# A graph network's last three aggregations: which chunks are fetched row by row, and by whom

## The chip, the cores and the metric

The program runs on one core of a Trainium2 chip. Its time is device microseconds; the number used is the median of three runs. An engine is named as the profile names it: PE (TensorE), PEld (its weight loads), DVE (VectorE), ACT (ScalarE), POOL (GpSimd), SP (SyncE); a q behind the name (ACTq, SPq) is that engine's queue of register, semaphore and DMA-issuing instructions.

## The reference, cut to what matters

3125 nodes with 256 features, 50000 edges sorted by destination. Two attention layers, an edge-attribute layer, then a relational layer and two hypergraph convolutions. The last three end in the same form: rows of a table, one for each edge, are fetched by the edge's source, weighted, and added up by destination.

```python
# relational layer: table rows are (source node, relation)
msg = h[edge_src] * edge_norm[:, None]
agg = jax.ops.segment_sum(msg, seg, num_segments=R * N)
# each of the two convolutions
h = jax.nn.relu(x @ w1 + b1)
msg = ew[:, None] * h[src]
agg = jax.ops.segment_sum(msg, dst, num_segments=x.shape[0])
h = agg @ w2 + b2
```

Both layers become: fetch 50000 rows of 256 floats from HBM (`rel_d` once, `feat_d` twice), and add them up per destination node.

## The kernel before, in words

**Tiling.** Edges are cut into chunks of 128; two chunks are a pair, and there are 196 pairs (`PAIRS`). A pair's rows land in one of 28 ring slots (`ring`, `RING`), edge p of a chunk in partition p. TensorE multiplies a pair by a 0/weight matrix that DVE makes, once for every destination tile that the pair touches: 220 steps (`T`) for 196 pairs. DVE adds each step's result to the tile's sum. In the last 21 or so steps PE also does the work of the layer that follows, for tiles that are finished (`pe_rows_late`, `pe_convolve_late`).

**Who fetches.** POOL walks the pairs (`gather_pairs`, L181) and issues one indirect DMA for each chunk (L186). For every pair from 28 on it waits until `slot_free` says that the slot is free; the wait for pair u is passed when ACT has begun its note of pair u - 25. In 12 of the pairs, 14, 28, ... 168 (`BY_ROW`), POOL fetches the first chunk alone; the second chunk's 128 rows are fetched one by one with plain DMAs of 1 KB (`fetch_row`, L203 to 207), rows 0 to 63 by SP (`sp_gather_rows`, L209) and rows 64 to 127 by ACT (`act_gather_rows`, L223). Each such engine first loads up to 32 row addresses (`ROW_REGS`) from SBUF into registers with one load (L219 on SP, L246 on ACT), and then issues one DMA for each.

**Notes.** For pairs 0 to 171 (`NOTES` = 172) ACT tells PE that a pair is there: it waits until the steps of an old pair are done (that number comes from `lastT`, of which L229 loads 14 entries, `LASTS`, every 14 pairs), frees the slot (L232), waits for the pair's landing and in a by-row pair for its 128 rows, and counts `pair_ready` up (L237). Behind each note it issues a share of the rows for the next by-row pair: 64 rows over 14 notes, the last of them right before that pair's own note. From pair 172 on POOL gives the notes itself (`pool_note`, L196), that of pair u - 2 behind the fetches of pair u; before the first of these, at pair 174, it waits until all of ACT's 172 notes are given (L199).

**SP.** For by-row pair number n it waits for the slot (as POOL does), and from n = 2 on for all rows of number n - 2 (L215), then loads and issues 64 rows. It has nothing else to do meanwhile.

The addresses of the rows lie in `row_rel` and `row_src`, one partition for each by-row pair, 128 four-byte entries in it; `lastT` is one row of four-byte entries. Row 64 of a chunk thus stands 256 bytes behind the start of its partition's addresses, and entry 14 of `lastT` 56 bytes behind its start.

Of the kernel before, what the change touches and what calls it, by code (L numbers as in the profile page):

```python
# [14 lines left out]
P = 128  # L15
# [22 lines left out]
BIG = 1.0e30  # L38
LN_EPS = 1e-5
BN_EPS = 1e-5  # L40
ROW_STEP = 14
NOTES = 172
PEEL = 2
SAFE = PAIRS
ACT_TILES = 10
BY_ROW = tuple(range(ROW_STEP, NOTES, ROW_STEP))
SP_ROWS = 64
ROW_REGS = 32
ROW = 4 * D
LASTS = 14  # L50
W_GAT = D + HEADS + 1
DX = D + 2 * HEADS
AW = 130
# [20 lines left out]
def pool_chunks(u, gat, by_row):  # L74

    return 1 if u in by_row or (u == PAIRS - 1 and not gat) else 2


class Signal:
# [7 lines left out]
def gnn_program(nc, t, out):  # L87
    life = ExitStack()

    def sb(name, shape, dt=F32, scope=None):  # L90
        return (scope or life).enter_context(nc.sbuf_tensor(name, shape, dt))
# [64 lines left out]
    class Steps:  # L156


        def __init__(self, tag, scope, gat, attr=None, signals=sem, by_row=()):
            self.gat, self.attr, self.width = gat, attr, W_GAT if gat else D  # L160
            self.by_row = by_row
            if by_row:
                self.rows_landed = [signals(f"{tag}_rows_landed{k}") for k in range(2)]
            self.hot_made = signals(tag + "_hot_made")
            self.pair_ready = signals(tag + "_pair_ready")
            self.step_done = signals(tag + "_step_done")
            self.slot_free = signals(tag + "_slot_free")
            self.added = signals(tag + "_added")
            if attr is not None:
                self.attr_hot_made = signals(tag + "_attr_hot_made")  # L170
                self.attr_ready = signals(tag + "_attr_ready")
                self.attr_done = signals(tag + "_attr_done")
                self.attr_added = signals(tag + "_attr_added")
                self.attr_landed = [signals(f"{tag}_attr_landed{k}") for k in range(4)]
            self.landed = []
            for u in range(PAIRS):
                at = pair_landed[u % RING]
                at.at += 16 * pool_chunks(u, gat, by_row)
                self.landed.append(at.at)

    def gather_pairs(pool, g, table, index, ring, pairs=range(PAIRS)):  # L181
        for u in pairs:
            if u >= RING:
                pool.wait_ge(g.slot_free, u - RING + 1 + RELEASE)
            for j in range(pool_chunks(u, g.gat, g.by_row)):
                pool.indirect_dma_start(  # L186
                    out=ring[:, u % RING, j, 0:D], out_offset=None, in_=table,
                    in_offset=bass.IndirectOffsetOnAxis(ap=index[:, u, j:j + 1], axis=0),
                ).then_inc(pair_landed[u % RING].sem, 16)
            if not g.gat and u - 2 >= NOTES:  # L190
                pool_note(pool, g, u - 2)
        if not g.gat:
            for u in range(PAIRS - 2, PAIRS):
                pool_note(pool, g, u)
# [8 lines left out]
    def fetch_row(eng, g, n, p, at, table, ring):  # L203

        row = bass.RuntimeValue.of_register_unchecked(at, min_val=0, max_val=(table.shape[0] - 1) * ROW)
        eng.dma_start(ring[p:p + 1, g.by_row[n] % RING, 1, 0:D].bitcast(U8),
                      table.rearrange("n f -> (n f)").bitcast(U8)[bass.ds(row, ROW)].unsqueeze(0))           .then_inc(g.rows_landed[n % 2], 16)

    def sp_gather_rows(sp, tag, g, table, index, ring):  # L209

        for n, u in enumerate(g.by_row):
            if u >= RING:
                sp.wait_ge(g.slot_free, u - RING + 1 + RELEASE)
            if n >= 2:
                sp.wait_ge(g.rows_landed[n % 2], 16 * P * (n // 2))  # L215
            for q in range(0, SP_ROWS, ROW_REGS):
                w = min(ROW_REGS, SP_ROWS - q)
                at = [sp.alloc_register(f"{tag}_at{n}_{q + k}") for k in range(w)]
# [4 lines left out]
    def act_gather_rows(act, tag, g, table, index, ring):  # L223

        lasts = [act.alloc_register(f"{tag}_last{k}") for k in range(LASTS)]
        done = act.alloc_register(f"{tag}_done")
        for u in range(NOTES):
            if u % LASTS == 0:
                act.reg_load(lasts, lastT[0:1, u:u + LASTS])  # L229
            act.reg_alu(done, lasts[u % LASTS], 1, ALU.max)  # L230
            act.wait_ge(g.step_done, done)
            act.sem_inc(g.slot_free, 1)  # L232
            act.wait_ge(pair_landed[u % RING].sem, g.landed[u])
            if u in g.by_row:
                n = g.by_row.index(u)
                act.wait_ge(g.rows_landed[n % 2], 16 * P * (n // 2 + 1))
            act.sem_inc(g.pair_ready, 1)  # L237
            n, share = u // ROW_STEP, u % ROW_STEP
            if n < len(g.by_row):
                rest = P - SP_ROWS  # L240
                for k in range(rest * share // ROW_STEP, rest * (share + 1) // ROW_STEP):
                    p = SP_ROWS + k
                    if k % ROW_REGS == 0:
                        w = min(ROW_REGS, P - p)
                        at = [act.alloc_register(f"{tag}_at{n}_{p + x}") for x in range(w)]
                        act.reg_load(at, index[n:n + 1, p:p + w])  # L246
                    fetch_row(act, g, n, p, at[k % ROW_REGS], table, ring)

    def ready_pairs(act, tag, g, ring):
        lasts = [act.alloc_register(f"{tag}_last{k}") for k in range(RING)]  # L250
# [162 lines left out]
    ring = sb("ring", [P, RING, 2, W_GAT], scope=gat)  # L413
# [25 lines left out]
    def carve(area, at, shape, dt=F32):  # L439

        size = 1
        for n in shape:
            size *= n
        size //= {BF16: 2, U8: 4}.get(dt, 1)
        flat = area[:, at:at + size]
        flat = flat if dt == F32 else flat.bitcast(dt)
        names = " ".join("abcd"[:len(shape)])
        return flat.rearrange(f"p ({names}) -> p {names}", **dict(zip("abcd", shape))) if len(shape) > 1 else flat
# [54 lines left out]
    rest = carve(arena_flat, 5490, (2 * HEADS * NT,))  # L503
# [1126 lines left out]
    def tail():  # L1630
# [272 lines left out]
        with nc.Block() as block:  # L1903
            @block.sync
            def _(sp):
                chunk = ROW_STEP * 2 * P
                for goal, ids in ((row_src, t["src"]), (row_type, t["type"])):
# [44 lines left out]
            @block.scalar  # L1952
            def _(act):
                act.wait_ge(s_row_at, 1)
                act_gather_rows(act, "agr", g_rel, rel_d, row_rel, ring)
                act.wait_ge(s_eps, 1)
                act_rows(act)
                for z, tag in enumerate(convs):
                    for k in range(5):
                        act.wait_ge(stored[k], 16 * 5 * (z + 1))  # L1960
                    act_gather_rows(act, f"ag{tag}", g_conv[z], feat_d, row_src, ring)
                    act_convolve(act, z)
                    act_sqrt(act, z, 0)
                    for r in range(NR):
                        act_norm(act, z, 0, r, s_n1[z], ACT.Relu)
                    act_sqrt(act, z, 1)
                    for r in range(NR):
                        act_norm(act, z, 1, r, s_n2[z], ACT.Identity if z else ACT.Relu)
                        if z == 1 and r >= 2:
                            for n in range(CH[r - 2][0] + 1, CH[r - 2][1], 2):  # L1970
                                act_odd(act, n)
                        if z == 0 and r >= 2:
                            for n in range(*CH[r - 2]):
                                act_rectify(act, 1, n)
                    if z == 0:
                        for n in range(CH[NR - 2][0], NT):
                            act_rectify(act, 1, n)
                for n in range(CH[NR - 2][0] + 1, NT, 2):
                    act_odd(act, n)
# [100 lines left out]
```

## Time and profile before

| what | value |
|---|---|
| three runs | 3306.64, 3307.64, 3316.96 us; median 3307.64 us |
| span of the profiled execution | 3318.0 us |
| busiest | POOL 2386.1 us (72%), PE 2189.3 us (66%), DVE 2090.3 us (63%), ACT 1413.4 us (43%) |
| mean granted TensorE clock | 0.844 |
| DMA | 466.05 MB, mean 140 GB/s |

The profile is one execution. The span is from its first to its last instruction; of the three runs the slowest lies nearest to it. The three aggregations that the change touches are three stretches of some 475 us each: 1765.8 to 2241 us, 2259.2 to 2734.5 us and 2789.8 to 3265 us. A row of the page's groups names line, engine, operation, what is written and read, the count, then busy time, mean ns of one, and the idle time before them with what ended it. Waiting, loading of registers and issuing of plain DMAs are not counted as busy, so ACT and SP look idle in these stretches; what their queues do is seen in the views of single lines and in the timeline.

### The profile page before, as it was taken

What the parts mean: (1) busy time and instruction counts of PE and PEld (TensorE: products, weight loads), DVE (VectorE), ACT (ScalarE), POOL (GpSimd) and SP (SyncE); (2) the same over time, 40 slices, a digit from 0 to 9 for tenths busy, and PEclk for the clock granted to TensorE, in tenths of its full rate; (3) what the DMA queues carried; (4) which work ended last, traced back from release to release, by engine and by line L of the source; (5) the groups of instructions that cost most, each with busy time, mean ns of one, the idle gap of its engine ahead of it and who ended that gap; (6) DMA issues with size and microseconds to landing.
All of it is one profiled execution on the core that took longest, in us unless ns stands there. A gap on an engine that the chain in (4) does not pass through costs nothing. (4 is left out here: it accounts for less than half of the span.)

```text
span 3318.0 us, 73877 instructions
## 1 busy us (share of the span) xinstructions
PE 2189.3 (66%) x11487; PEld 1592.8 (48%) x11488; DVE 2090.3 (63%) x5467; ACT 1413.4 (43%) x4736; POOL 2386.1 (72%) x2419
## 2 busy tenths in 40 slices
PE   6566377776656367766696666676666677666667
PEld 2455255555455355555443444454444456444446
DVE  8899867766489967776694444464444454444446
ACT  2666399998566479988581000031000014000004
POOL 7877777777777767777655777775777773777773
PEclk9799699998889789999797778687777798777788
DMA  5488734443688745443694333443333332333332
GB/s 165 132 228 226 215 111 141 140 127 105 174 227 227 214 118 163 142 130 104 161 283 159 109 109 109 125 125 108 109 109 109 108 104 78 110 109 110 109 107 79
DMA packets 346744, 466.05 MB, mean 140 GB/s; under 512 B 111879, under 2 KB 262248, under 8 KB 343184
## 3 DMA queue, kind: packets, MB, share of 16 engines
q0 software_dynamic: 111952, 284.59, 29.8%
q1 hardware_dynamic: 161584, 111.23, 11.5%
q10 hardware_dynamic: 72852, 67.08, 7.5%
q14 instruction: 328, 2.69, 0.3%
q8 instruction: 28, 0.46, 0.1%
HBM read 385.50 MB, written 76.97 MB: 139 GB/s over the span
## 5 line engine op out<-in xcount | busy, mean ns | idle before, releaser
L400 PE MATMUL t_ps<-t_ring,shared 128*128 x2640 | 900.5, 494 | 499.2 <-ACTq L237 418.3
L400 PEld LDWEIGHTS t_ps<-t_ring,shared 128*128 128x128 f32 x2640 | 601.8, 244 | 787.5 <-issue 697.4
L186 POOL DMA_INDIRECT ring<-feat_d,srcC x784 | 772.3, 985 | 264.8 <-issue 215.2
L186 POOL DMA_INDIRECT t_ring<-feat_d,srcC x758 | 719.7, 950 | 289.3 <-issue 215.5
L265 ACT ACTIVATE ring<-ring,exC 128x64 f32<-128x64 f32 x3136 | 788.0, 335 | 0.2
L400 PE MATMUL bank<-ring,arena 128*128 x1408 | 426.9, 428 | 166.7 <-ACT ring L265 117.8
L318 DVE TENSOR_TENSOR acc<-acc,t_ps 128x256 f32 x440 | 185.3, 421 | 504.3 <-PE t_ps L400 502.9
L608 POOL DMA_INDIRECT attr_d<-abuf,attr_pos x392 | 401.9, 1025 | 117.7 <-issue 117.7
L186 POOL DMA_INDIRECT t_ring<-rel_d,relC x379 | 360.0, 950 | 160.6 <-issue 107.4
L302 DVE TENSOR_SCALAR shared<-lane,dlocT,weightT 128x128 f32<-128x128 f32 x1320 | 406.4, 360 | 50.9 <-issue 31.9
L1828 ACT COPY t_ring<-t_pt 128x512 f32<-128x512 f32 (+1 forms) x14 | 7.8, 554 | 883.3 <-PE t_pt L1795 883.3
L400 PEld LDWEIGHTS bank<-ring,arena 128*128 128x128 f32 x1408 | 258.5, 204 | 240.0 <-issue 213.3
L1036 PE MATMUL wide<-arena 128*128 128x100 bf16 x4704 | 258.0, 215 | 173.5 <-ACT arena L952 157.9
L1036 PEld LDWEIGHTS wide<-arena 128*128 128x128 bf16 x4704 | 232.6, 102 | 199.5 <-DVE arena L997 118.3
L296 DVE TENSOR_TENSOR arena<-lane,dlocT 128x256 f32<-128x256 f32 x440 | 185.0, 420 | 91.1 <-issue 53.4
L318 DVE TENSOR_TENSOR X<-X,t_ps 128x256 f32 x220 | 92.5, 420 | 234.0 <-PE t_ps L400 232.7
L318 DVE TENSOR_TENSOR acc<-acc,bank 128x261 f32 x352 | 150.2, 427 | 117.0 <-PE bank L400 108.4
L948 ACT ACTIVATE arena<-arena,minus_part 128x512 bf16<-128x512 bf16 x196 | 141.4, 721 | 146.9 <-issue 116.2
L1003 DVE TENSOR_TENSOR arena<-wide,shared 128x800 f32<-128x800 f32 x196 | 191.2, 976 | 8.9 <-PE wide L1036 8.2
L1768 ACT ACTIVATE rstd<-mv,t_eps 128x1 f32<-128x1 f32 x25 | 7.1, 284 | 439.1 <-DVE mv L1737 439.1
L1012 DVE TENSOR_REDUCE shared<-arena 128x800 f32 (+1 forms) x196 | 190.4, 971 | 0.1
L390 PEld LDWEIGHTS bank<-arena 128*128 128x128 f32 x704 | 139.8, 202 | 70.1 <-issue 45.3
(297 smaller groups left out, 2715.3 us busy)
## 6 DMA issues: line engine op xcount, KB each, us to landing
arena<-lo_d ACTq DMA_DIRECT2D x392, 128.0 KB
rel_d<-mid_stage SPq DMA_DIRECT2D x25, 1024.0 KB, 4.7
arena<-attr_d SPq DMA_DIRECT2D x98, 260.0 KB, 2.9
abuf<-in_attr SPq DMA_DIRECT2D x56, 448.0 KB
t_ring<-feat_d SPq DMA_DIRECT2D x1536, 1.0 KB
t_ring<-feat_d ACTq DMA_DIRECT2D x1536, 1.0 KB
ring<-feat_d,srcC POOLq DMA_INDIRECT x784
t_ring<-rel_d SPq DMA_DIRECT2D x768, 1.0 KB
```

Of the source, the lines that this page charges most:

```text
L186: pool.indirect_dma_start(out=ring[:, u % RING, j, 0:D], out_offset=None, in_=table, in_offset=bass.IndirectOffsetOnAxis(ap=index[:, u, j: ...
L265: last = act.activation(part_of_row, part_of_row, ACT.Copy, scale=exC[:, bass.ds(u, 1), j, h])
L296: last = dve.tensor_tensor(hot[:, k % NHOT, :, :], lane[:, :].unsqueeze(1).to_broadcast([P, 2, P]), dlocT[:, bass.ds(s, 1), :].rearrange(" ...
L302: last = dve.tensor_scalar(hot[:, k % NHOT, j, :], lane[:, :], dlocT[:, bass.ds(s, 1), j], weightT[:, bass.ds(s, 1), j], ALU.is_equal, ALU ...
L318: dve.tensor_tensor(acc[:, tile, 0:g.width], acc[:, tile, 0:g.width], ps[k % len(ps)][:, 0:g.width], ALU.add).then_inc(g.added, 1)
L390: pe.matmul(ps_a[k % NHOT][:, 0:AW - 1], hot_a[:, k % NHOT, :], aring[:, slot, 0:AW - 1], start=True, stop=True).then_inc(g.attr_done, 1)
L400: last = pe.matmul(ps[k % len(ps)][:, 0:g.width], hot[:, k % NHOT, j, :], ring[:, slot, j, 0:g.width], start=(j == 0), stop=(j == 1))
L608: pool.indirect_dma_start(out=attr_d, in_=abuf[:, g % BUFS, k, :], in_offset=None, out_offset=bass.IndirectOffsetOnAxis(ap=attr_pos[:, c:c ...
L948: act.activation(apart[:, k % 2, :], lo[:, k, 1, :], ACT.Abs, bias=minus_part[:, 0:1])\
L1003: dve.tensor_tensor(cand[:, k % 2, :, :, :], pk[k % 2][:, :, :].rearrange("p b (s x) -> p (b s) x", x=P)[:, :, 0:HEADS * NT] .rearrange("p ...
L1012: dve.tensor_reduce(e[:, bass.ds(4 * c, 4), :], cand[:, k % 2, :, :, :].rearrange("p (j q) h n -> p j h q n", q=2), AX.XY, ALU.add).then_i ...
L1036: last = pe.matmul(pk[k % 2][:, j // 2, at:at + HEADS * NT], looked[:, k % 2, q, j * P:(j + 1) * P], tab[:, piece, q * HEADS * NT:(q + 1) ...
```

## The change

By-row pairs are every 12th: 12, 24, ... 168, 14 of them where there were 12, so POOL issues 377 fetches in an aggregation where it issued 379. Of a chunk's 128 rows SP fetches rows 0 to 69 and ACT rows 70 to 127. ACT spreads its 58 rows over the 12 notes that end four notes ahead of the by-row pair's own note (`ROW_LEAD`), and those of the first by-row pair over notes 0 to 7. `lastT` is loaded 16 entries at a time. Addresses are still loaded up to 32 at a time, from the first row that the engine fetches: on SP three loads a chunk (32, 32 and 6, from rows 0, 32 and 64), on ACT two (32 and 26, from rows 70 and 102).

```diff
--- before.py
+++ after.py
@@ -38,16 +38,17 @@
 BIG = 1.0e30
 LN_EPS = 1e-5
 BN_EPS = 1e-5
-ROW_STEP = 14
+ROW_STEP = 12
 NOTES = 172
 PEEL = 2
 SAFE = PAIRS
 ACT_TILES = 10
 BY_ROW = tuple(range(ROW_STEP, NOTES, ROW_STEP))
-SP_ROWS = 64
+SP_ROWS = 70
+ROW_LEAD = 4
 ROW_REGS = 32
 ROW = 4 * D
-LASTS = 14
+LASTS = 16
 W_GAT = D + HEADS + 1
 DX = D + 2 * HEADS
 AW = 130
@@ -74,6 +75,17 @@
 def pool_chunks(u, gat, by_row):
 
     return 1 if u in by_row or (u == PAIRS - 1 and not gat) else 2
+
+
+def act_rows(by_row, u):
+
+    rest = P - SP_ROWS
+    for n in range(len(by_row)):
+        first = max(0, ROW_STEP * n - ROW_LEAD)
+        pairs = ROW_STEP * (n + 1) - ROW_LEAD - first
+        for k in range(rest):
+            if first + k * pairs // rest == u:
+                yield n, k
 
 
 class Signal:
@@ -235,16 +247,13 @@
                 n = g.by_row.index(u)
                 act.wait_ge(g.rows_landed[n % 2], 16 * P * (n // 2 + 1))
             act.sem_inc(g.pair_ready, 1)
-            n, share = u // ROW_STEP, u % ROW_STEP
-            if n < len(g.by_row):
-                rest = P - SP_ROWS
-                for k in range(rest * share // ROW_STEP, rest * (share + 1) // ROW_STEP):
-                    p = SP_ROWS + k
-                    if k % ROW_REGS == 0:
-                        w = min(ROW_REGS, P - p)
-                        at = [act.alloc_register(f"{tag}_at{n}_{p + x}") for x in range(w)]
-                        act.reg_load(at, index[n:n + 1, p:p + w])
-                    fetch_row(act, g, n, p, at[k % ROW_REGS], table, ring)
+            for n, k in act_rows(g.by_row, u):
+                p = SP_ROWS + k
+                if k % ROW_REGS == 0:
+                    w = min(ROW_REGS, P - p)
+                    at = [act.alloc_register(f"{tag}_at{n}_{p + x}") for x in range(w)]
+                    act.reg_load(at, index[n:n + 1, p:p + w])
+                fetch_row(act, g, n, p, at[k % ROW_REGS], table, ring)
 
     def ready_pairs(act, tag, g, ring):
         lasts = [act.alloc_register(f"{tag}_last{k}") for k in range(RING)]
```

## Rows read from the trace of the kernel before

**Rows 1.** Busy time by stretch: the three aggregations (the first and the third; columns as in the first row).
```profile
core 0: us, PE busy (x) PEld busy (x) DVE busy (x) ACT busy (x) POOL busy (x), PEclk, DMA share, GB/s
1765.70:2241.10 475.40, 315.48 (x969) 216.59 (x970) 223.34 (x738) 26.25 (x91) 359.97 (x379) 0.77 0.40 115
2789.70:3265.00 475.30, 315.19 (x969) 216.99 (x970) 210.51 (x670) 10.04 (x20) 359.82 (x379) 0.77 0.38 108
```

**Rows 2.** Line 186 (POOL) in the third aggregation: one line's view, durations in ns.
```profile
L186 POOL DMA_INDIRECT t_ring<-feat_d,srcC x379: 942/947/1031, 2789.8 to 3264.0; - x190
  issue: 107.7, 353
```

**Rows 3.** The same view, only as far as pair 174.
```profile
L186 POOL DMA_INDIRECT t_ring<-feat_d,srcC x338: 942/947/1031, 2789.8 to 3212.5; - x169
```

**Rows 4.** Who waited for whom: total us, times, longest us.
```profile
PE t_ps L400 <- ACTq L237: 418.3, 236, 10.7
POOL t_ring L186 <- ACTq L232: 22.0, 72, 0.3
...
SPq L219 <- ACTq L232: 250.6, 33, 10.4
```

**Rows 5.** Chain that ended last, around the end of the third aggregation: start, us, what.
```profile
3246.50 0.95 POOL t_ring L186
...
3249.31 1.12 PE t_ps L400 x4
...
3276.16 0.48 ACT t_ring L1837
```

**Rows 6.** Line 237 (ACT notes) at both ends of the third aggregation.
```profile
L237 ACTq EVENT_SEMAPHORE  x1: 17/17/17, 2793.8 to 2793.8; - x1
...
L237 ACTq EVENT_SEMAPHORE  x2: 17/17/17, 3205.2 to 3207.8; - x2
```

**Rows 7.** Line 206 (row fetches) in the third aggregation.
```profile
L206 ACTq DMA_DIRECT2D t_ring<-feat_d x768: 227/228/544, 2796.2 to 3200.3; - x192
```

**Rows 8.** Timeline of ACT's queue, three short stretches: start us, us, what, count.
```profile
2338.26 1.50 ACTq L206 DMA_DIRECT2D t_ring<-feat_d  x5
...
2353.24 3.01 ACTq L206 DMA_DIRECT2D t_ring<-feat_d  x9
...
2336.53 1.10 ACTq L206 DMA_DIRECT2D t_ring<-feat_d  x3
```

**Rows 9.** Timeline of SP's queue, one chunk, then its second half.
```profile
2343.51 23.27 SPq L206 DMA_DIRECT2D t_ring<-feat_d  x64
...
2356.52 10.26 SPq L206 DMA_DIRECT2D t_ring<-feat_d  x32
```

**Rows 10.** Line 229 (14 registers each): all, then four single loads.
```profile
L229 ACTq TENSOR_LOAD <-lastT x39: 1228/1577/3477, 1767.7 to 3200.6; - x39
...
L229 ACTq TENSOR_LOAD <-lastT x1: 3317/3317/3317, 1804.6 to 1804.6; - x1
...
L229 ACTq TENSOR_LOAD <-lastT x1: 1507/1507/1507, 1839.8 to 1839.8; - x1
...
L229 ACTq TENSOR_LOAD <-lastT x1: 3312/3312/3312, 3167.0 to 3167.0; - x1
...
L229 ACTq TENSOR_LOAD <-lastT x1: 1515/1515/1515, 3200.6 to 3200.6; - x1
```

**Rows 11.** Other register loads: 4, 20, 28, 32 and 32 registers each.
```profile
L362 DVEq TENSOR_LOAD <-tiles x5: 345/347/355, 842.9 to 3262.2; - x5
...
L381 PEldq TENSOR_LOAD <-slots x55: 1357/1362/1582, 409.4 to 3223.2; - x55
...
L253 ACTq TENSOR_LOAD <-lastT x14: 1717/1738/1931, 412.2 to 1543.7; - x14
...
L219 SPq TENSOR_LOAD <-t_row_src x48: 2024/2119/2281, 2258.5 to 3155.7; - x48
...
L246 ACTq TENSOR_LOAD <-t_row_src x48: 1968/2066/2162, 2263.3 to 3184.9; - x48
```

## The prediction

> **What bounds the kernel now.** I read the busy time by stretch first. In each of the three aggregations POOL is the busiest engine at 360 of 475 us, PE follows at 309 to 315, and ACT looks idle [rows 1]. Then the view of POOL's own line. Its 379 fetches start between 2789.8 and 3264.0 us, one every 474.2 / 378 = 1.2545 us. A fetch takes 0.947 us, and the 353 gaps behind "issue" are 107.7 / 353 = 0.305 us each, which adds up to the same 1.252 us [rows 2]. So POOL never stops, and an aggregation lasts 379 x 1.2545 = 475.4 us plus a tail. The waits agree. POOL's 22.0 us behind ACT's slot count are 72 times 0.3 us, the ordinary gap under another name; SP by contrast waits 250.6 us for slots, and PE waits 418.3 us for ACT's notes, since it is fed at POOL's pace [rows 4]. The chain shows POOL up to some 3249 us, then PE until ACT takes over at 3276.2 [rows 5]. That last stretch of PE work (late steps and the next layer's products) hangs on POOL's last pairs and is not touched, so the tail stays as it is.
>
> The views of single lines show the second thing to be read: how near ACT's queue is to POOL's pace. It counts as idle and is not. In the third aggregation its first note ends at 2793.8 and its last at 3207.8 [rows 6], that is 4.0 and 418.0 us after POOL's start. POOL's own first note comes behind pair 174, at 338 x 1.2545 = 424 us [rows 3]; there it waits until ACT is through. ACT now arrives 6 us before that. This is the point where a late ACT turns into a late POOL.
>
> **What the queue steps cost.**
> Row fetch on ACT: five DMAs span 1.50 us, and the last is 0.23 long, so the pitch is (1.50 - 0.23) / 4 = 0.318 us [rows 7, 8]. Nine with a note between them span 3.01 us, so a note that has nothing to wait for costs 3.01 - 0.23 - 8 x 0.318 = 0.24 us; other such stretches give 0.22, and I take 0.225 [rows 8]. The first fetch behind a load takes longer: three span 1.10 us in place of 0.87, 0.23 us more [rows 8].
> Row fetch on SP: (10.26 - 0.23) / 31 = 0.324 us; with its load in the middle a chunk of 64 takes 23.27 us [rows 9].
> Register loads: 4 registers take 0.35 us, 20 take 1.36, 28 take 1.74, 32 take 2.0 to 2.15 [rows 11]. That is about 0.25 us for every four.
> The 14-register load of line 229 does not fit. Of its 39 executions 21 take 1.23 to 1.60 us and 18 take 3.29 to 3.48, and they alternate: 3317, 1507 ... 3312, 1515 ns [rows 10]. They differ in nothing but the address. The quick ones begin 0, 112, 224 ... bytes into the row, the slow ones 56, 168 ... bytes, and these are 8 more than a multiple of 16. My reading: from an address that is a multiple of 16 four registers are read at a time (14 are then three fours and two single ones, five reads, as 20 registers are five fours). From any other address each register is read alone, at 3.315 / 14 = 0.237 us. All loads of rows 11 begin at multiples of 16 (20 registers are 80 bytes, 28 are 112, rows 32, 64 and 96 stand at 128, 256 and 384 bytes).
> The Trainium skill, page "Runtime: NRT & Kernel Launch", section "Instruction fetch mechanics", says that a load into sequencer registers costs about 200 ns a register even in bulk. The slow loads agree (0.237 us), the aligned ones do not (0.065 us). With 0.20 for 0.237 the sum below would be 14 x 58 x 0.037 = 30 us smaller an aggregation, some 3481 us in all.
>
> **The change part by part.**
> POOL: two fetches fewer an aggregation, 2 x 1.2545 = 2.5 us, three times 7.5 us. This is all that can be gained while POOL is the bound.
> lastT 16 at a time: entries 0, 16, 32 ... stand at multiples of 64 bytes, so 11 loads of four fours, between 1.0 and 1.5 us, taken as 1.1 (between the rows of 4 and of 20 registers, nearest to the latter). Before, 13 loads averaged some 2.4 us. It saves about 19 us of ACT's queue.
> SP: 70 x 0.325 + 2.05 + 2.14 for two loads, about 0.8 for the one of 6 registers at row 64 (256 bytes, three reads), 0.2 for the rest: 28 us a chunk. By-row pairs come every 23 fetches x 1.2545 = 28.9 us. SP keeps up just so. It starts up to 25 pairs early, and even 2.1 us for the short load (29.3 us, 0.4 us lost a chunk) stays inside that lead. Cost: nothing; that lead hides it.
> ROW_LEAD: the last row comes four notes before its pair's note, so the note no longer waits for it. That moves waiting off ACT only.
> ACT's address loads: this is what decides. Its rows now begin at 70, 280 bytes in, and at 102, 408 bytes in. Both are 8 more than a multiple of 16. No row of the trace shows 32 registers from such an address. From below the price is that of an aligned load, 2.06 us [rows 11]; next comes that price plus the whole difference of line 229 as a fixed toll, 2.06 + 1.8 [rows 10]; from above it is each register alone at 0.245. I take each alone at 0.237, because that one rule gives all five sizes of rows 10 and 11: 32 x 0.237 = 7.6 and 26 x 0.237 = 6.2 us, 13.7 us a chunk where 4.1 were.
>
> **The sum.** ACT from POOL's first fetch to its last note, when it never waits: 4.0 to the first note; 14 x 58 = 812 rows x 0.318 = 258.2; 28 first fetches x 0.23 = 6.4; 14 x 13.74 = 192.4; 10 further lastT loads x 1.1 = 11.0; 171 notes x 0.225 = 38.5. Together 510.5 us. The same sum for the kernel before (768 rows, 24 loads of 2.06, six lastT loads of 3.3 and six of 1.5) gives 371, and its last note is at 418.0, so 47 us of waiting for landings are in there. They are slack, and a late ACT doesn't have them.
> POOL comes to its own first note behind 336 fetches, at 421.5 us, and stands until 510.5. (From about pair 90 on it will also be held by the ring, when ACT is some 24 pairs late; that time is inside the same 89 us.) Then 41 fetches x 1.2545 = 51.4 us follow: 561.9 against 475.4, 86.5 us more an aggregation, 259.5 us for three. By pairs: ACT needs 18.4 + 0.5 + 13.7 + 0.8 + 2.7 = 36.2 us for 12 pairs, POOL 28.9. The stretch behind pair 175 runs at POOL's pace as before, so PE's tail is the same.
> The differences go onto the median: 3307.6 + 259.5 = 3567 us. Against the span of the profiled execution, which is 10.4 us above the median, it would be 3577.5.
>
> **The rivals.**
> 1. Each register alone (the forecast). Single reads of 0.225 to 0.245 us and a pitch of 0.318 to 0.33 give 225 to 300 us more: 3533 to 3608. Chance 0.82.
> 2. The bad address costs a toll on each load and not a toll on each register. ACT's sum with aligned prices is 510.5 - 192.4 + 14 x 4.0 = 374; each us of toll adds 28. POOL is held only beyond 421.5, so from a toll of 1.7 us on. At 1.8 it is 424.6: POOL loses 3.1 and gains 2.5, some 3310 us. At 4 it is 486, 3494 us. For it speaks that only one size was seen at such an address; against it that 3.3 / 14 meets the price that two leftover registers need in rows 10. Chance 0.07.
> 3. Not slower: the address of rows 70 and 102 costs nothing. ACT then needs 26.5 us for 12 pairs against POOL's 28.9, its last note is at some 415 us, before POOL's 421.5, and POOL stays the bound. The time is 3307.6 - 7.5 = 3300.1 us, 0.23% faster. It decides at a load price below 3.7 us in the mean. Against it stand 18 loads of 18. Chance 0.09.
> 4. SP falls behind and holds ACT's notes, because row fetches from both queues at once slow down. At 0.36 us a row SP would need 30.5 us a chunk, 1.6 too much, and ACT's notes would end 20 us late: 3340 us if alone. SP's pitch beside ACT's is 0.324 and steady. Chance 0.02.
>
> **How the numbers follow.** The forecast is case 1, 3567 us. Its bounds and the skill's price for a register give 3481 to 3608; with half of case 2 above the lower end, and room for instruction fetches on a queue that now never rests, the range is 3480 to 3620 and leaves out case 3, most of case 2 and case 4. About 0.3% (10 us) is what a measurement here can tell from no change. Faster by more needs case 3 with something on top: 0.02. Within it: the rest of case 3 and the lowest part of case 2, 0.09. Slower: 0.89.
>
> **What would show it.** L246 at 7.6 and 6.2 us, and L229 near 1.1, all alike. L206 on ACT at an unchanged pitch. ACT's last note 510 us behind POOL's first fetch. POOL's line with waits for L232 of tens of us and one long wait for the notes, at pair 175, and otherwise the same 1.2545 us. SP waiting for slots more than now. PE waiting for L237 some 200 us more. The prediction is wrong if L246 stays near 2 us (then case 3), or takes 4 (case 2), or if POOL waits nowhere.

## The result, and the profile after

The changed kernel takes 3586.7 us (3583.87 to 3588.71 in four runs), the kernel before 3307.1 us (3306.03 to 3316.96 in four). The ratio is 1.0835, with a 95% interval of 1.0814 to 1.0855: 279.6 us slower. The forecast was 3567 us, in a range of 3480 to 3620.

The page of the changed kernel: its span, the busy time of the engines, and the costliest group with the idle time ahead of it.

```profile
span 3583.0 us, 75473 instructions
PE 2173.2 (61%) x11487; PEld 1579.8 (44%) x11488; DVE 2090.6 (58%) x5467; ACT 1413.3 (39%) x4736; POOL 2377.8 (66%) x2413
L409 PE MATMUL t_ps<-t_ring,shared 128*128 x2640 | 885.2, 488 | 791.7 <-ACTq L249 711.2
```

No engine is busy for longer than before by more than 0.3 us. PE's matmuls in the aggregations wait 711.2 us for ACT's notes where they waited 418.3 [rows 4]. The busy time by stretch says how long the first and the third aggregation last from POOL's first fetch to its last:

```profile
core 0: us, PE busy (x) PEld busy (x) DVE busy (x) ACT busy (x) POOL busy (x), PEclk, DMA share, GB/s
1753.90:2322.00 568.10, 309.51 (x971) 211.91 (x972) 223.93 (x738) 26.63 (x91) 357.71 (x377) 0.75 0.34 96
2962.70:3530.80 568.10, 309.86 (x969) 212.51 (x970) 211.01 (x669) 10.04 (x20) 357.40 (x377) 0.75 0.31 91
```

568.1 us where it was 475.4 [rows 1], with the same work in it: POOL busy 357.4 us in place of 359.8. The three stretches add 3 x 92.6 = 278 us, which is the whole of the loss. The stretch before the first aggregation is outside the change, and the two profiled executions differ there by some 12 us the other way, so their spans are only 265 us apart.

The view of POOL's line, now 198, in the third aggregation (durations in ns; below it what ended the engine's idle time, us and times), then the same up to pair 174 and from pair 175 on:

```profile
L198 POOL DMA_INDIRECT t_ring<-feat_d,srcC x377: 940/946/1033, 2962.8 to 3529.8; - x189
  issue: 103.4, 339
  ACTq L244: 61.8, 35
  POOLq L213: 45.0, 1
...
L198 POOL DMA_INDIRECT t_ring<-feat_d,srcC x336: 940/946/1033, 2962.8 to 3433.8; - x168
...
L198 POOL DMA_INDIRECT t_ring<-feat_d,srcC x41: 940/946/972, 3479.7 to 3529.8; - x41
```

A fetch still takes 0.946 us and the ordinary gap is still 0.305 us. Two waits are new. The 35 waits for line 244, the slot count that ACT gives, take 61.8 us where 0.3 us each would be 10.7, 51 us more. And one wait of 45 us stands between the 336th fetch and the 337th. Less the two fetches saved this is 51 + 45 - 2.5, some 93 us, the growth of the stretch. The timeline of POOL shows it (start, length, what, and in brackets the idle time ahead and its releaser):

```profile
3432.51 0.94 POOL L198 DMA_INDIRECT t_ring<-feat_d,srcC  x1 [0.30 <-issue]
3433.76 0.95 POOL L198 DMA_INDIRECT t_ring<-feat_d,srcC  x1 [0.30 <-issue]
3479.70 0.94 POOL L198 DMA_INDIRECT t_ring<-feat_d,srcC  x1 [44.99 <-POOLq L213]
3480.94 0.95 POOL L198 DMA_INDIRECT t_ring<-feat_d,srcC  x1 [0.30 <-issue]
```

Line 213 is POOL's own first note, at pair 174; in front of it POOL waits until all 172 of ACT's notes are given (line 211). The first of ACT's notes and the last three, in the view of line 249, and under them ACT's row fetches:

```profile
L249 ACTq EVENT_SEMAPHORE  x1: 17/17/17, 2966.9 to 2966.9; - x1
...
L249 ACTq EVENT_SEMAPHORE  x3: 17/17/17, 3476.3 to 3478.9; - x3
...
L218 ACTq DMA_DIRECT2D t_ring<-feat_d x812: 227/228/534, 2974.0 to 3472.6; - x163
```

The first note ends 4.1 us behind POOL's first fetch at 2962.8, the last 516.1 us behind it. Before, it was 418.0 [rows 6]. POOL goes on 0.8 us later and needs its 41 fetches as ever. What keeps ACT is in its register loads. These are one load of 32 row addresses and one of 26, then all 28 of the third aggregation, then the 33 lastT loads of all three:

```profile
L255 ACTq TENSOR_LOAD <-t_row_src x1: 6899/6899/6899, 2967.0 to 2967.0; - x1
...
L255 ACTq TENSOR_LOAD <-t_row_src x1: 5864/5864/5864, 2985.3 to 2985.3; - x1
...
L255 ACTq TENSOR_LOAD <-t_row_src x28: 5837/6390/7099, 2967.0 to 3455.5; - x28
...
L241 ACTq TENSOR_LOAD <-lastT x33: 1035/1307/1342, 1755.9 to 3464.1; - x33
```

Where a load of 32 took 2.07 us [rows 11] this one takes 6.9; the median of all 42 of its size is 7.07, that of the 42 of 26 registers 5.90. The lastT load, whose 14-register form went up to 3.48 us every second time [rows 10], is never above 1.35.

The waits, longest in total, of POOL, PE and SP (us in total, times, longest):

```profile
POOL t_ring L198 <- ACTq L244: 179.0, 99, 4.6
POOL t_ring L198 <- POOLq L213: 134.7, 3, 45.0
...
PE t_ps L409 <- ACTq L249: 711.2, 213, 10.7
...
SPq L231 <- ACTq L244: 274.6, 33, 10.4
```

### The profile page after: what moved, and what is told of

Its sections match the earlier page's. It is cut to its first block and busy times, and to the rows that moved or that the text cites. A ratio compares the mean times of both kernels' runs of the same rounds, so it can differ in the third digit from the quotient of the medians.

```text
span 3583.0 us, 75473 instructions
## 1 busy us (share of the span) xinstructions
PE 2173.2 (61%) x11487; PEld 1579.8 (44%) x11488; DVE 2090.6 (58%) x5467; ACT 1413.3 (39%) x4736; POOL 2377.8 (66%) x2413
## 5 line engine op out<-in xcount | busy, mean ns | idle before, releaser
L409 PE MATMUL t_ps<-t_ring,shared 128*128 x2640 | 885.2, 488 | 791.7 <-ACTq L249 711.2
L409 PEld LDWEIGHTS t_ps<-t_ring,shared 128*128 128x128 f32 x2640 | 588.6, 241 | 1078.5 <-issue 996.3
L327 DVE TENSOR_TENSOR X<-X,t_ps 128x256 f32 x220 | 92.6, 421 | 326.7 <-PE t_ps L409 325.2
```

Source lines behind the costliest of these rows:

```text
L327: dve.tensor_tensor(acc[:, tile, 0:g.width], acc[:, tile, 0:g.width], ps[k % len(ps)][:, 0:g.width], ALU.add).then_inc(g.added, 1)
L409: last = pe.matmul(ps[k % len(ps)][:, 0:g.width], hot[:, k % NHOT, j, :], ring[:, slot, j, 0:g.width], start=(j == 0), stop=(j == 1))
```

## The experiments

Names: `a_` starts from the changed kernel, `b_` from the kernel before, `c_` is a further version. Each ratio is against the kernel before on the same chip. Its median there was 3311.4 us for `a_aligned`, `a_half`, `b_act8` and `b_sp8`, 3310.5 for `probe`, `b_lasts16`, `a_lead0` and `c_11`, and 3309.2 for `probe2`, `b_step12` and `c_68`.

### Is it the address of ACT's loads, and nothing else?

`a_aligned`: the same rows on the same engines behind the same notes, but the loads begin at entries 68 and 100.

```diff
-                if k % ROW_REGS == 0:
-                    w = min(ROW_REGS, P - p)
-                    at = [act.alloc_register(f"{tag}_at{n}_{p + x}") for x in range(w)]
-                    act.reg_load(at, index[n:n + 1, p:p + w])
-                fetch_row(act, g, n, p, at[k % ROW_REGS], table, ring)
+                if p == SP_ROWS or p in (68, 100):
+                    lo = max(x for x in (68, 100) if x <= p)
+                    w = min([x for x in (68, 100) if x > p] + [P]) - lo
+                    at = [act.alloc_register(f"{tag}_at{n}_{lo + x}") for x in range(w)]
+                    act.reg_load(at, index[n:n + 1, lo:lo + w])
+                fetch_row(act, g, n, p, at[p - lo], table, ring)
```

> The changed kernel with one thing different: ACT loads the addresses of its rows from entries 68 and 100 (272 and 400 bytes in, multiples of 16; 32 and 28 registers) and leaves the two it doesn't need unused. Same rows, same engines, same notes. Theory (each register is read alone from an address that is no multiple of 16, and ACT's queue thereby holds POOL): loads near 2 us in place of 7.0 and 5.9, ACT's sum 4 + 273 for rows + 56 for loads + 13 + 45 = 391 us, below POOL's 421.5, so POOL is the bound with two fetches fewer: 3307.1 - 7.5 = 3299.6 us. Rival (the 14th by-row chunk, 58 rows over 8 notes at the start, or SP at 28 of 28.9 us hold POOL by themselves): the time stays well above before, 3330 us or more, though the loads are short.

Measured: 3302.7 us, ratio 0.9974 (0.9964 to 0.9983). Its loads of two convolutions, and POOL's line in the third aggregation:

```profile
L256 ACTq TENSOR_LOAD <-t_row_src x56: 1909/2026/2196, 2255.1 to 3165.5; - x56
...
L198 POOL DMA_INDIRECT t_ring<-feat_d,srcC x377: 942/946/1032, 2780.1 to 3251.5; - x189
  issue: 106.2, 348
  ACTq L244: 8.2, 27
```

The loads take 2.0 us, and POOL waits for nothing again: 27 gaps of 0.3 us behind the slot count are the ordinary gap. The other parts of the change together with good addresses make the kernel 0.26% faster, 8.8 us against the kernel before on the same chip, where 7.5 were reckoned for six fetches of POOL. So the whole loss of 280 us, and the gain of 9 us besides, hangs on two addresses. Entries 68 and 100 stand at odd multiples of 16 bytes (272 and 400), so 16 is enough; 32 isn't needed. SP now has as little room as ACT: it works without a pause, one chunk every 28.7 us, where POOL reaches the next by-row pair every 28.9.

`a_half`: as `a_aligned`, with loads at entries 70 (30 registers) and 100 (28): `(68, 100)` becomes `(70, 100)`.

> The changed kernel with one of ACT's two loads put right: 30 registers from entry 70 (280 bytes, not a multiple of 16), 28 from entry 100 (400 bytes, a multiple). Theory: 6.6 + 1.9 = 8.5 us a chunk in place of 12.98, so ACT's last note comes 14 x 4.5 = 63 us earlier, at 453 us, still behind POOL's 421.5; each us of it is a us of POOL: 3586.7 - 3 x 63 = 3398 us. Rival (a load from such an address costs a toll beyond a threshold, or POOL's loss isn't proportional to ACT's lateness): not half of the loss goes, or nearly all.

Measured: 3414.2 us, ratio 1.0317 (1.0301 to 1.0332). POOL's wait for the notes:

```profile
POOL t_ring L198 <- POOLq L213: 110.4, 3, 37.6
...
POOL t_ring L198 <- ACTq L244: 21.4, 70, 0.3
```

This is 16 us above the 3398 us expected. ACT's last note comes at 457 us, not 453, which is 12 of the 16 over three aggregations. POOL's idle time at pair 175 is 37 us; less the two fetches, three times 34.5 us is 103 us, the loss against the kernel before on the same chip (102.8). So the loss is proportional to ACT's lateness. Beyond that single wait POOL isn't held: the 70 gaps behind the slot count are the ordinary 0.3 us.

### Does it need the rest of the change?

`b_act8`: the kernel before, with only ACT's loads cut otherwise, by the same code as above with `(64, 66, 98)`.

> The kernel before, 12 by-row chunks of 64 rows on ACT, with ACT's loads cut otherwise: 2 registers from entry 64, 32 from entry 66 (264 bytes), 30 from entry 98 (392 bytes). Nothing else of the change is in it. Theory: 0.6 + 7.0 + 6.6 = 14.2 us a chunk where 4.2 were, 12 x 10 = 120 us onto the 371 to 385 us that ACT needs without waiting: last note near 505 us, 81 us behind POOL's 424: 3307.1 + 3 x 82 = 3553 us, 3530 to 3570. Rival (the loss belongs to every 12th pair or to the 58 rows ahead of time, and addresses only add to it): 3307 to 3400 us.

Measured: 3586.9 us, ratio 1.0841 (1.0825 to 1.0858). ACT's loads in the convolutions, POOL's waits, and the notes' line:

```profile
L247 ACTq TENSOR_LOAD <-t_row_src x72: 494/6749/7214, 2347.1 to 3457.6; - x72
...
POOL t_ring L186 <- POOLq L201: 156.3, 3, 52.2
POOL t_ring L186 <- ACTq L232: 146.0, 81, 6.5
...
L237 ACTq EVENT_SEMAPHORE  x516: 17/17/1992, 1760.9 to 3479.0; - x172
```

So the loss is there without any other part of the change. It is 34 us above the 3553 us expected and outside the 3530 to 3570, 11 us an aggregation. The notes' line says where most of that is: the wait of a note for something that has not landed goes up to 1992 ns. The kernel before fetches its last rows right before their own note, and the landing of those rows is waited for even when ACT is late; I had reckoned ACT as never waiting. Of the 36 by-row notes 15 waited 1.1 to 2.0 us, and all notes of an aggregation took some 8 us more than where nothing of ACT's own is awaited. The remainder is in terms that the sum had a little too small, as told below for the sum of the prediction.

### Does it matter which engine loads slowly?

`b_sp8`: the same cuts for SP.

```diff
-            for q in range(0, SP_ROWS, ROW_REGS):
-                w = min(ROW_REGS, SP_ROWS - q)
+            for q, w in ((0, 2), (2, 32), (34, 30)):
```

> The kernel before, with the same 10 us a chunk put on SP and not on ACT: 2 registers from entry 0, 32 from entry 2 (8 bytes), 30 from entry 34 (136 bytes). Theory: SP then needs 35.5 us a chunk where by-row pairs come every 33.9, so it is late by 1.6 us a chunk from the third chunk on, 14 us at the last; ACT waits for those rows at pair 168 and its last note comes near 430 us, 6 us behind POOL's 424: 3307.1 + 3 x 6 = 3325 us, against some 3553 for the same load cost on ACT. Rival (load time costs the same wherever it stands, for instance because it takes SBUF's port from POOL): 3500 us or more.

Measured: 3320.4 us, ratio 1.0027 (1.0015 to 1.0039). SP's loads in the convolutions:

```profile
L218 SPq TENSOR_LOAD <-t_row_src x72: 635/6359/6834, 2254.1 to 3193.2; - x72
```

Some 10 us a chunk more cost 2 to 3 us an aggregation on SP (477.4 us from first fetch to last in the mean, before 475.3) and 92 on ACT. That is 9 us in all where 18 were expected: ACT did wait for SP's last rows, but its last note came at 424.5 to 426 us and not at 430. A slow load costs what its queue has no room for. SP had some 8 us a chunk to spare and may start up to 25 pairs ahead of a by-row pair, and behind ACT's loads stand the notes that everybody waits for.

### What does a load cost?

A first try added 48 loads with unused results to SP's queue. They are not in its trace, so it measured nothing but the kernel before over again (3307.4 us).

> The kernel before with 48 register loads more on SP, behind its last row fetch, where it only waits for the output: 1, 2, 4, 8, 16 and 32 registers from entries 0, 1, 2, 3, 4, 8, 12 and 16 of an address row. Theory: from entries 0, 4, 8, 12 and 16 (multiples of 16 bytes) a load reads four registers at a time, 0.25 us a read, so 32 registers take 2.0 us; from entries 1, 2 and 3 each register takes 0.21 to 0.24 us, so 32 take 7 us and 4 take 0.9. Rival a: only the address modulo 8 or 4 matters (entry 2 differs from 1 and 3). Rival b: leading registers are read alone until a multiple of 16 is reached, so that entries 1 to 3 cost under 1 us more at any size. The time of the kernel should not move, since SP has some 130 us to wait there.

`probe2` puts the addresses to use: SP's rows are loaded in another cut for each by-row pair (the eight cuts come around again with the ninth).

```diff
-            for q in range(0, SP_ROWS, ROW_REGS):
-                w = min(ROW_REGS, SP_ROWS - q)
+            cuts = [(0, 1, 33), (0, 3, 35), (0, 2, 6, 14, 30, 62), (0, 1, 5, 13, 29, 61), (0, 3, 7, 15, 31, 63),
+                    (0, 4, 12, 28, 60), (0, 32), (0, 2, 34)][n % 8] + (SP_ROWS,)
+            for q, w in [(a, b - a) for a, b in zip(cuts, cuts[1:])]:
```

> The kernel before with SP's rows loaded in other cuts, another for each by-row pair, so that loads of 1 to 34 registers begin at entries of all four remainders: for number 0 at entries 0, 1, 33; 1 at 0, 3, 35; 2 at 0, 2, 6, 14, 30, 62; 3 at 0, 1, 5, 13, 29, 61; 4 at 0, 3, 7, 15, 31, 63; 5 at 0, 4, 12, 28, 60; 6 at 0, 32; 7 at 0, 2, 34. The addresses are in use, which those of the first such try were not (its 48 loads had no user and are not in its trace). Theory: at a multiple of 16 bytes 4, 8, 16, 32 registers take 0.35, 0.6, 1.1 to 1.3, 2.0 us; at remainders of 4, 8 and 12 bytes alike some 0.21 us a register: 0.9, 1.8, 3.5, 6.9 us. Rival a: the remainder of 8 differs from 4 and 12. Rival b: the registers up to the next multiple of 16 are read alone and the others by four, under 1 us more at any size. The time of the kernel is secondary: SP has 8 us to spare a chunk and spends up to 11 more in seven of twelve, so 3307 to 3330 us.

Measured: 3306.7 us in a single run, as much as before within the spread. The view of the loads' line, seven loads of the second aggregation: 4, 8, 16 and 32 registers from entries 2, 6, 14 and 30, then 8, 16 and 32 from entries 4, 12 and 28.

```profile
L220 SPq TENSOR_LOAD <-t_row_src x1: 1152/1152/1152, 2318.0 to 2318.0; - x1
...
L220 SPq TENSOR_LOAD <-t_row_src x1: 1927/1927/1927, 2320.5 to 2320.5; - x1
...
L220 SPq TENSOR_LOAD <-t_row_src x1: 3531/3531/3531, 2325.5 to 2325.5; - x1
...
L220 SPq TENSOR_LOAD <-t_row_src x1: 6747/6747/6747, 2334.3 to 2334.3; - x1
...
L220 SPq TENSOR_LOAD <-t_row_src x1: 795/795/795, 2428.0 to 2428.0; - x1
...
L220 SPq TENSOR_LOAD <-t_row_src x1: 1312/1312/1312, 2431.5 to 2431.5; - x1
...
L220 SPq TENSOR_LOAD <-t_row_src x1: 2216/2216/2216, 2438.1 to 2438.1; - x1
```

All 156 loads together, medians by the remainder of the address (entry modulo 4) and the number of registers, in ns:

| registers | entry mod 4 = 0 | 1 | 2 | 3 |
|---|---|---|---|---|
| 4 | 520 | 1092 | 1149 | 1123 |
| 8 | 795 | 1948 | 1932 | 1928 |
| 16 | 1237 | 3580 | 3539 | 3535 |
| 32 | 2129 | 6763 | 6745 | 6753 |

From 8 to 32 registers an aligned load grows by 1334 ns, 0.22 us for every four registers; the others grow by 4813 to 4825 ns, 0.20 us for each. Both rivals fall: the remainders of 4, 8 and 12 bytes cost alike, and the load doesn't read its way to the next multiple of 16 first. The Trainium skill's page "Runtime: NRT & Kernel Launch", section "Instruction fetch mechanics", gives some 200 ns a register; this is the slope of the loads that start anywhere else, and four registers for that price is what an aligned start gives here. The Trainium skill's page "SBUF — State Buffer", section "Specifications (TRN2)", tells of lines of 16 bytes, the same unit; that the loader reads in such lines is my reading and is shown by no run.

### What are the other parts worth?

`b_lasts16`: the kernel before with `LASTS = 16`.

> The kernel before with the lastT loads of the change alone: 16 entries every 16 notes. Theory: 11 loads of 1.33 us where 13 averaged 2.45 take 17 us off ACT's queue, which then waits those 17 us longer for landings; POOL is the bound, so the time stays at 3311 within 3 us. Rival (ACT's queue holds something up in the kernel before as well): up to 3 x 17 us faster, 3260.

Measured: 3309.9 us, ratio 0.9999 (0.9989 to 1.0008): no difference that can be told, as expected, on a queue that has time to spare.

`b_step12`: the kernel before with `ROW_STEP = 12`.

> The kernel before with the chunk count of the change alone: every 12th pair, rows split 64 and 64 (so ACT's loads stay on multiples of 16 bytes), the last rows right before the note, lastT 14 at a time. Theory: ACT needs 4 + 896 rows x 0.336 + 28 x 2.1 + 29 + 45 = 437 us, and some 1.5 us of landing at each of 14 by-row notes: 458 us, 37 behind POOL's 421; 3310.5 + 3 x (37 - 2.5) = 3414 us. So the split, the lead and the lastT loads are what makes room for the two more chunks. Rival (they do nothing, as each alone does nothing on the kernel before): 3303 us.

Measured: 3422.8 us, ratio 1.0347 (1.0331 to 1.0363). POOL waits at its first note:

```profile
POOL t_ring L186 <- POOLq L201: 120.7, 3, 43.5
```

Two more chunks with the old split and the old loads cost 114 us, 9 more than expected, and ACT's last note comes at 463.5, 457 and 459 us. What makes the two chunks free is the rest of the change, with good addresses. Against `a_lead0` below, which differs from this run in the split and in the lastT loads, the row fetches take 27 us more of ACT's queue an aggregation and the lastT loads 16, and the last note comes some 37 us later. Of these parts only the lastT loads were put into the kernel before alone, and were worth nothing there; for the split that wasn't tried.

`a_lead0`: `a_aligned` with `ROW_LEAD = 0`.

> The changed kernel with aligned loads on ACT (as in a_aligned, 3302.7 us) and ROW_LEAD = 0: the last of ACT's rows again right before its pair's own note. Theory: ACT waits some 1.5 us for these rows at each of 14 by-row notes, about 21 us of the 26 us that it has to spare in an aggregation, so its last note comes at 415 to 421 us, not behind POOL's 421.1: 3303 us, unchanged within 4 us. Rival (the lead is what keeps ACT ahead of POOL): 10 to 40 us slower.

Measured: 3308.5 us, ratio 0.9995 (0.9986 to 1.0004), 5.9 us above `a_aligned` (6.8 if each is taken against the kernel before on its own chip). The notes' line of all three aggregations:

```profile
L249 ACTq EVENT_SEMAPHORE  x516: 17/17/3842, 1760.3 to 3201.6; - x172
```

A note now waits up to 3.8 us, and the 14 by-row notes of an aggregation together wait 29 to 31 us where 21 were expected. ACT's last note comes at 425.1, 421.6 and 422.0 us, up to 4 us behind POOL, which is there at 421 to 421.6. So the spare time was more than used up, and the lead is worth some 6 us; I had expected it to be just free.

### Versions

`c_68`: the changed kernel with `SP_ROWS = 68`.

> The changed kernel with one number changed: 68 rows on SP in place of 70, so that ACT's 60 rows begin at entries 68 and 100, 272 and 400 bytes in. Theory: ACT's sum rises by 28 rows x 0.336 = 9 us over a_aligned's, out of 26 us to spare; POOL stays the bound: 3303 us as a_aligned, 0.26% below the kernel before. Rival (ACT is too near its limit with 60 rows): POOL waits at pair 175 by a few us, 3306 to 3315.

Measured: 3303.3 us, ratio 0.9981 (0.9970 to 0.9992). This can't be told from `a_aligned`, and nothing is changed but the number; ACT's last note comes at 415 us, so 60 rows still fit.

`c_11`: `ROW_STEP = 11`, `SP_ROWS = 68`, `LASTS = 20`.

> A version further along: every 11th pair (15 chunks by row), 68 rows on SP and 60 on ACT, so that ACT's loads begin at entries 68 and 100 (multiples of 16 bytes), lastT 20 entries at a time, lead 4. ACT by its measured prices: 4 + 15 x (60 x 0.336 + 2 x 2.05) + 8 x 1.4 + 171 x 0.26 = 424 us, with less stray time 420; POOL comes to its first note behind 335 fetches at 420. Theory: POOL saves three fetches, 3.8 us an aggregation, and loses 0 to 4 us again to ACT: 3299 to 3312 us, at best 4 us below a_aligned and at worst even with the kernel before. Rival (there is more slack than the sums say): 3300 us or less, with no wait of POOL at pair 175.

Measured: 3335.2 us, ratio 1.0077 (1.0064 to 1.0091). POOL's wait for the notes is back:

```profile
POOL t_ring L198 <- POOLq L213: 39.3, 3, 16.9
```

ACT's last note came at 436, 430 and 430 us where the sum said 420 to 424. In the first aggregation the rows took 303.5 us (302.4 reckoned), the loads 63.2 (61.5), lastT 12.8 (11.2) and the notes 52.1 (44.5). Of these 52.1 us 5.05 are a single wait for a landing, in front of the note of by-row pair 165; what was late there no run shows. In the other two aggregations no note waited. There the rows took 302 to 304 us, the loads 63, lastT 13 and the notes 46 to 48, so that small excesses add up to the 6 us. My discount for less stray time was wrong as well. At this split 15 chunks are more than ACT can carry, and 14 are not. SP is past its pace too: it takes 27.5 us a chunk, and by-row pairs come every 21 fetches, 26.3 us.

## Why the prediction was right, step by step

**What bounds the kernel**: right. POOL's pace is unchanged at 1.25 us a fetch, ACT's queue was the second limit, and its point of contact is pair 175.

**The addresses**: right, and this decided it. The rule was read off 18 slow loads of 14 registers and held at 32 and 26. Its size was 6% too high: 0.237 us a register contained the fixed part of a load. `probe2` gives 0.20 a register and some 0.35 fixed on SP; on ACT 32 and 26 registers took 7.1 and 5.9 us, 0.3 above that, where I had 7.6 and 6.2. The toll (rival 2) would have left 32 registers near 3.9 us. Taken over 14 chunks the loads are 181.8 us in place of 192.4.

**The sum**: 510.5 us against 516.1 for ACT's last note. Four terms were off, by the third aggregation's instructions from each one's start to the next one's: loads 10.6 us too much; rows 272.5 us against 264.6, since 0.318 is the undisturbed pitch and the mean with all pauses is 0.336; notes 44.3 against 38.5, 0.26 each and not 0.225; lastT loads 13.4 against 11.0, 1.3 us each and not 1.1. The median of a repeated step was taken where the sum needed its mean. That and 0.8 us until POOL moves again make 6 us an aggregation, 19 of the 20 us by which 3567 is below 3586.7. That it came so near is in part luck: the loads were put too high and the three others too low. With the loads alone put right the sum would have given 3535 us.

**POOL's two fetches, 7.5 us**: right, shown by `a_aligned` (8.8 us, interval 6 to 12 us).

**SP costs nothing**: right. Its third load took 1.0 us and not 0.8, it waits 274.6 us for slots where it waited 250.6, and `a_aligned` shows that 70 rows fit, at 28.7 us a chunk of 28.9.

**ROW_LEAD costs and brings nothing**: its cost is nothing, but it does bring something. When ACT is late or nearly so, the landing of its own last rows is real time: 6 us in `a_lead0`, part of the 34 us in `b_act8`. The sentence that the 47 us of waiting before are slack was too general: those for POOL's fetches are, those for ACT's own rows are not. They were also fewer: with the mean prices of the changed kernel the kernel before needs 385 us and not 371, and 33 us are left.

**The ring**: POOL was held by the slot count too, as said, from the 182nd fetch on, which is pair 94. As the prediction put it, that time is no addition: what the ring takes, the wait at pair 175 is shorter by, since ACT's last note sets the end of both.

**Rival 3** (no cost, 3300 us) is what `a_aligned` and `c_68` measure once the addresses are put right: forecast and rival differed in the price of one load and in nothing else.

**The figures of the range**: 3481 us should have been 3477 by the prediction's own terms, and the bounds of case 1, 3533 and 3608, should have been 3538 and 3616. None of this moves the result in or out of the range. Of the signs named ahead, PE's added waiting for the notes was put too low, at some 200 us: it is 293.

## What to carry to other kernels

A queue that the profile counts as idle can be some 90% full (here 385 of 418 us) with register loads, DMA issues and notes. Add its instructions up, by their mean and not by their median, before it gets more to do. When a table of addresses is cut between engines, cut it where each load starts on a multiple of 16 bytes: here 70 in place of 68 cost 283 us. A slow load costs only where the queue behind it has no room, so look who waits for the next instruction on that queue.

## What the runs showed of the hardware

In `probe2` a load of sequencer registers from SBUF takes 0.22 us for every four registers if its first byte stands at a multiple of 16, and 0.20 us for every single one if not, whichever of the three other remainders of four-byte entries it is; the fixed part is some 0.35 us. 32 registers are 2.1 or 6.75 us on SP, and 2.1 (`a_aligned`) or 7.1 us (the changed kernel) on ACT. A one-register load takes 0.44 to 0.70 us. The 48 loads of `probe`, whose registers nobody uses, are not in its trace. Row fetches of 1 KB issued from SP and ACT side by side kept a pitch of 0.32 us each, with pauses that bring the mean to 0.336 on ACT.
